# Toeplitz weight blocks loaded once and copied to the second image's rows on GpSimd

## The reference

```python
qkv = _conv(x, w_qkv)                                        # 768 channels
agg = _conv(_conv(qkv, w_dw, groups=C3), w_pw, groups=3 * DIM)
qkv = jnp.concatenate([qkv, agg], axis=1)
...
vk = jnp.einsum('bhds,bhes->bhde', v, k)
out = jnp.einsum('bhde,bhes->bhds', vk, q)
```

## Time and profile before

| | before |
|---|---|
| median of 3 runs | 2079.17 us (2075.14 to 2084.48) |
| profiled execution | 2083.96 us, span of its instructions 2082.1 us |
| PE busy | 1786.3 us (86%) |
| DVE busy | 1372.3 us (66%) |
| ACT busy | 901.7 us (43%) |
| POOL (GpSimd) busy | 277.0 us (13%) |
| mean granted TensorE clock | 0.945 |
| DMA | 267.17 MB in 199916 packets |

### The profile page before, as it was taken

The page is one execution under the profiler, slowest core; times in us unless marked ns, Lnnn a source line. Parts: engine busy times, 40 slices in busy tenths (PEclk is TensorE's granted clock), DMA queues, the critical chain, the costliest instruction groups (busy, mean ns, idle before and its releaser), DMA issues. The chain is left out here.

```text
span 2082.1 us, 42128 instructions
## 1 busy us (share of the span) xinstructions
PE 1786.3 (86%) x16164; PEld 1195.1 (57%) x16164; DVE 1372.3 (66%) x2786; ACT 901.7 (43%) x2341; POOL 277.0 (13%) x189
## 2 busy tenths in 40 slices
PE   2699999999999999997877888999983499999998
PEld 1355555555555555565555666666661366666666
DVE  4677777666555556442333447777875899999994
ACT  0344454454554544453433445455541144444343
POOL 1000000001111101002111110000001233333331
PEclk9899999999999999998988899999995699999999
DMA  3112222237666667479988986545513001111101
GB/s 100 39 63 78 101 94 78 78 125 185 207 170 199 201 160 215 145 185 218 237 231 219 246 229 166 134 121 149 156 48 128 16 32 63 62 63 63 47 32 47
DMA packets 199916, 267.17 MB, mean 128 GB/s; under 512 B 108516, under 2 KB 159588, under 8 KB 199720
## 3 DMA queue, kind: packets, MB, share of 16 engines
q1 hardware_dynamic: 189320, 225.68, 38.4%
q10 hardware_dynamic: 10240, 38.54, 6.0%
q0 software_dynamic: 160, 0.26, 0.0%
HBM read 148.84 MB, written 115.61 MB: 127 GB/s over the span
## 5 line engine op out<-in xcount | busy, mean ns | idle before, releaser
L499 DVE TENSOR_TENSOR vk<-p_vk,mask_vo 128x512 f32<-128x512 f32 x256 | 176.4, 689 | 478.3 <-PE p_vk L392 478.3
L426 PE MATMUL p_dw<-tw,q 98*64 98x98 f32 x3072 | 198.3, 266 | 86.8 <-ACT agg_out L694 34.9
L834 POOL COPY q<-qd 98x768 f32<-98x768 f32 x128 | 110.5, 900 | 1085.5 <-DMA qd<-qkv_scratch 787.2
L667 ACT ACTIVATE half_b<-p_qkv 98x384 f32<-98x384 f32 x256 | 134.2, 524 | 244.2 <-PE p_qkv L351 229.6
L426 PEld LDWEIGHTS p_dw<-tw,q 98*64 98x64 f32 x3072 | 148.1, 143 | 151.5 <-issue 67.8
L694 ACT ACTIVATE agg_out<-p_dw 128x294 f32<-128x294 f32 x256 | 106.9, 417 | 258.6 <-PE p_dw L426 246.0
L452 PE MATMUL p_g<-o,w_proj 128*128 128x392 f32 x512 | 207.5, 531 | 3.4 <-DVE var L555 2.8
L351 PE MATMUL p_qkv<-w_qkv,half_a 128*98 128x384 f32 x512 | 193.8, 502 | 6.7 <-DVE half_a L571 6.7
L351 PE MATMUL p_qkv<-w_qkv,z_odd 128*98 128x384 f32 x512 | 190.2, 494 | 1.8 <-DVE z_odd L571 1.8
L404 PE MATMUL p_out<-vk,qr 128*49 128x136 f32 x2048 | 170.5, 287 | 8.5 <-DVE oN L514 5.4
L711 ACT ACTIVATE o<-p_turn 128x196 f32<-128x196 f32 x256 | 85.5, 334 | 167.5 <-PE p_turn L413 166.1
(11 more groups left out here) (192 smaller groups left out, 3202.4 us busy)
## 6 DMA issues: line engine op xcount, KB each, us to landing
qkv_scratch<-half_b SPq DMA_DIRECT2D x32, 1176.0 KB
qd<-qkv_scratch SPq DMA_DIRECT2D x64, 588.0 KB
agg_scratch<-agg_out ACTq DMA_DIRECT2D x128, 294.0 KB, 5.8
tw<-in_w_toep SPq DMA_DIRECT2D x128, 220.5 KB
half_a<-agg_scratch SPq DMA_DIRECT2D x48, 392.0 KB, 6.9
half_b<-agg_scratch SPq DMA_DIRECT2D x48, 392.0 KB, 6.8
half_a<-in_x SPq DMA_DIRECT2D x16, 784.0 KB, 4.9
x_scratch<-xb SPq DMA_DIRECT2D x16, 784.0 KB, 4.8
```

The source lines that it names most:

```text
L426: mm = pe.matmul(p_dw[NP * cp:NP * cp + NP, PR * s:PR * s + PR], q2[:, U % Q2, DB_CH * cp + 3 * (f % DB_FILLS) + s, :, :].rearrange("r w q ...
L499: v.tensor_tensor(dst[:, :, 0:128].rearrange("p k (c n) -> p k c n", c=HC), src[:, :, 0:2 * D].unsqueeze(2).to_broadcast([128, 4, HC, 2 * D]),
L667: a.activation(raw[:, e, g % 4, :, r], p_qkv[r][0:PR, 0:QKV], ACT.Copy).then_inc(raw_ev, 1)
L834: g.tensor_copy(q2[:, U % Q2, DB_CH * cp:DB_CH * cp + DB_CH, :, :].rearrange("r n w q -> r w n q"), qd[:, :, at:at + DB_CH, :]).then_inc(q ...
```

## The change

The second image's rows move from partitions 49 to 97 to partitions 64 to 112 (P2 = 113), in qd, q2 and tw. The rows 49 to 63 between them are zeroed once in tw and in qd, and the gathers copy the zeros of qd along. tw is loaded for the first image only, by two DMAs instead of four; GpSimd copies it to rows 64 to 112 (`pool_second`) and PE waits for that copy. Each of the four parts of qd is loaded by two DMAs of 49 rows, since its rows are no longer contiguous. GpSimd's order becomes: gather U+2, then the copy for U; at the start of each half three gathers stand ahead of the first copy.

```diff
+P2 = 64 + S
...
-        qd = sb("qd", [PR, NP // 2, QB_CH, 2])
-        q2 = sb("q2", [PR, Q2, 2 * DB_CH, NP // 2, 2])
-        tw = sb("tw", [PR, 2, 2, SB_CH, S])
+        qd = sb("qd", [P2, NP // 2, QB_CH, 2])
+        q2 = sb("q2", [P2, Q2, 2 * DB_CH, NP // 2, 2])
+        tw = sb("tw", [P2, 2, 2, SB_CH, S])
...
-                pe.wait_ge(tw_in[SB % 2], 64 * (SB // 2 + 1))
+                pe.wait_ge(tw_ok, SB + 1)
...
-            sp.dma_start(qd[:, w0:w1, :, :], qt[h][:, w0:w1, QB_CH * qb:QB_CH * qb + QB_CH, :]).then_inc(qd_in, 16)
+            for i in range(2):
+                sp.dma_start(qd[64 * i:64 * i + S, w0:w1, :, :],
+                             qt[h][S * i:S * i + S, w0:w1, QB_CH * qb:QB_CH * qb + QB_CH, :]).then_inc(qd_in, 16)
...
-                g.wait_ge(qd_in, 16 * QD_PARTS * (U // per + 1))
+                g.wait_ge(qd_in, 32 * QD_PARTS * (U // per + 1))
...
-            for i in range(2):
-                for p0, p1 in ((0, S - 1), (S - 1, S)):
-                    sp.dma_start(tw[S * i + p0:S * i + p1, SB % 2, i, :, :],
-                                 ins["w_toep"][p0:p1, SB_CH * sb_:SB_CH * sb_ + SB_CH, :]).then_inc(tw_in[SB % 2], 16)
+            for p0, p1 in ((0, S - 1), (S - 1, S)):
+                sp.dma_start(tw[p0:p1, SB % 2, 0, :, :],
+                             ins["w_toep"][p0:p1, SB_CH * sb_:SB_CH * sb_ + SB_CH, :]).then_inc(tw_in[SB % 2], 16)
+
+        def pool_second(g, SB):
+
+            g.wait_ge(tw_in[SB % 2], 32 * (SB // 2 + 1))
+            wait(g, q2_ok, 2 * min(SB + 3, FILLS // DB_FILLS * (SB // (FILLS // DB_FILLS) + 1)))
+            g.tensor_copy(tw[64:P2, SB % 2, 1, :, :], tw[0:S, SB % 2, 0, :, :]).then_inc(tw_ok, 1)
+            g.wait_ge(tw_ok, SB + 1)
...
-            sp.wait_ge(blank_ok, 1)
+            sp.wait_ge(blank_ok, 2)
...
             g.memset(tw[:, :, :, :, :], 0.0).then_inc(blank_ok, 1)
-            for U in range(2 * FILLS // DB_FILLS):
-                pool_gather(g, U)
+            g.memset(qd[:, :, :, :], 0.0).then_inc(blank_ok, 1)
+            g.wait_ge(blank_ok, 2)
+            per = FILLS // DB_FILLS
+            for U in range(2 * per):
+                if U % per == 0:
+                    pool_gather(g, U)
+                    pool_gather(g, U + 1)
+                if U % per + 2 < per:
+                    pool_gather(g, U + 2)
+                pool_second(g, U)
```

More of the change, by code:

```diff
@@ L262, in layer_one_phase @@
         qd_in, q2_ok = sem("qd_in"), sem("q2_ok")
-        tw_in = [sem("tw_in0"), sem("tw_in1")]
+        tw_in, tw_ok = [sem("tw_in0"), sem("tw_in1")], sem("tw_ok")
         agg_st = [sem("agg_st0"), sem("agg_st1")]
```

## The result

The changed kernel takes 2172.34 us (median of four runs, 2166.09 to 2173.32) against 2080.28 us for the kernel before (2075.14 to 2084.48): a ratio of 1.0455, 95% interval 1.0426 to 1.0484. Slower, as forecast, by 92 us where 142.5 were worked out; the time lies in the stated range of 2125 to 2310 us. The profiled execution spans 2170.9 us against 2082.1, 88.8 us more, and that difference is what the following lines account for.

The account below looks back on a forecast made before the run. PE bounds the first half; in the second, a chain of qd load and the Toeplitz load queued behind it stops PE. Terms 7 + 36 + 14.5 + 71 + 14 = 142.5 us slower gave 2222 us, range 2125 to 2310.

Parts of the forecast that it names:

- Part 3: qd loads: 49-row DMAs use the same seven engines each time, where 98 rows use 14; DMA share about half of 0.97.
- The price of the halving: Each qd load: transfer time doubles at half the engines, +9.9 us, bounds 8.7 and 16.9.
- Second half: Fills 128 to 255: seven chains of qd load, Toeplitz load and copy, 10.2 us longer each, 71 us (54 to 120).
- First half: Fills 0 to 127: longer chains less the distances before, 36 us (20 to 85), plus 14 us for new stalls.
- The clock term: PE in the first half: six new stalls of 3.9 us or more cost 14 us (0 to 20).
- The starts: First products of the halves wait for longer qd load, three gathers and a copy: 7 us and 14.5 us.
- Part 2: GpSimd's copies to the second image's rows: 1.3 us each, bounds 1.0 and 2.4, counting only on the chain.
- part 1: Toeplitz load halved, 220.5 KB less for each of 64 blocks: -1.0 us in each chain, bounds -2.0 and 0.
- The signs: Gather 4Q 25 to 32 us behind first qd issue; second-half PE waits at fill 16Q-8 15 to 20 us.
- (a): qd loads spread evenly or halves on different engines, load as fast as before: +7, 2086 us, no change; chance 0.10.
- (b): As (a), and lighter Toeplitz traffic removes PE's waits in the second half: -30, 2049 us; chance 0.04.
- (c): Seven engines, but the slower qd load mostly hidden, a third of 142.5 us stays: +48, 2127 us; chance 0.06.

Follow-up runs that it names:

- e1: Kernel before, with only each 98-row qd load cut into two of 49 rows, no copy: 2179.02 us, 1.0502.
- e2: Kernel before, with QD_PARTS 8 instead of 4, so as many qd loads as the changed kernel but of 98 rows: 2073.87 us, 0.9986.
- e9: Kernel before, with each qd load cut into 77 and 21 rows: 2114.54 us, 1.0152.
- e6: Kernel before, with each qd load cut into 96 and 2 rows: 2083.56 us, 1.0029.
- e3: Changed kernel, with qd loads cut into 48 + 48 + 2 rows, copy on GpSimd kept: 2094.38 us, 1.0093.
- e5: Changed kernel with 48 + 48 + 2 row qd loads, no copy, both Toeplitz blocks loaded by DMA, GpSimd's order as before: 2090.40 us, 1.0085.
- e4: Changed kernel without the copy: both Toeplitz blocks loaded by DMA, GpSimd's order as before, 49-row qd loads kept: 2173.96 us, 1.0470.

## Why the prediction was right, and where its sizes were off

**Part 3, seven engines: right.** The forecast share of "about half of 0.97" came as 0.49, and e1, e2 and e9 show that neither the count of DMAs nor the copy does it. The trace also counts the engines: the semaphore that qd's loads raise has 960 updates by DMA for the 64 loads before, 15 each, and 1024 for the 128 loads of the changed kernel, 8 each; e9 has 20 for each pair of 77 and 21 rows, e6 19 for 96 and 2, e3 35 for 48, 48 and 2. In the first load before, one update of each DMA comes 0.1 to 0.2 us behind its issue and ahead of its data. Read as that one for a DMA on fewer than 16 engines, and one more for each engine, these counts are 14, 7, 11 + 7, 16 + 2 and 16 + 16 + 2 engines. That both halves use the same seven follows from the rate: 145 GB/s is half of 278. The shares agree with the counts, at 0.07 for each engine: 0.97 for 14 (98 rows), 0.76 for 11 (77 + 21 rows) and 0.49 for 7. When the forecast was made, the trace had only the 0.97 beside 1.07 and 1.14; that 98 rows go to 14 engines and 49 to 7, in equal shares, was my estimate from it, and the counts bear out the numbers of engines. The shares over 1 are overlap in the records, as said there: up to 24 packets run at one time in the stretches of qd alone of e5 and e6, on 16 engines.

**The price of the halving: too high.** The term was +9.9 us a load. Alone it was +8.4 (21.1 against 12.7), below even my lower bound of 8.7; inside the second half, where I had put the upper end at 16.9, it was +7.0 (mean 25.6 against 18.6 of the seven). The term that was mis-sized is the part that doesn't double, put at 2.8 us from a load of 1 KB. By the updates of qd's semaphore the first and the fourth DMA before had landed at 458.58 and 465.00 us, 2.14 us apart for each; four such are 8.6 us of the 12.7, so 4.1 don't double. Doubling 8.6 gives the +8.4 (e1, with nothing but the cut, had +9.5). Inside the second half e1 and e4, which still load both images' blocks, have +8.3 and +8.4 in the mean; the changed kernel's +7.0 is 1.4 less, which fits its lighter Toeplitz traffic but isn't isolated by a run. The upper end of the sum, 17.2 us a chain, was added up from 16.9 and the middle values of the other two parts; by their own bounds it is 19.3, and nothing measured comes near it.

**Second half: 43.5 us for 71.** A group takes 47.4 us instead of 40.3 (fills 144 to 240: 1026.5 to 1310.9 now, 985.5 to 1227.5 before), +7.1 for each of six chains. The seventh, the first in time (fills 128 to 144), grows by 1.1 us only, since the gathers done ahead of the first product let the next qd load be issued 1.7 us behind it instead of 4.8, and its Toeplitz trail is 3.0 us for 4.4. The other terms cancelled as in the sum: the Toeplitz trail behind qd is no longer 1.1 to 5.9 us but 3.0 in five of seven groups, which is the gather and the copy (1.62 and 1.16 us), and 3.6 and 3.7 in the other two (1196.59 to 1200.23 above), where tw landed a little later. The order of GpSimd that I costed at nothing does set this trail, but its mean of 3.2 is that of before.

**First half: 21.6 us for 36 + 14.** The new waits add up to 20.3 us in seven groups (0.0, 7.8, 0.0, 3.4, 7.0, 1.8, 0.3), since the loads grew by 4.8 us in the mean and not by 9.9. The group with the least distance before, 3.3 us, waits 7.0 us, and that with 12.7 us not at all, as the slack says; the second, with 8.4 us, waits most, since its load grew by 10.0 us (16.2 to 26.2). The clock term of 14 us was too high, and no run shows it: the earlier trace rows has one stretch of 7 us at 0.66 behind one stall of 10.0 us, and nothing there or in a run gives what a stall of 3.9 us costs. The runs showed in its place a clock of 0.95 for 0.97 and 6.5 us more of busy PE; the granted clock reads 0.5 for 43.9 us of these products where it read 0.5 for 23.9 before. The same products, fills 0 to 124, before and after:

```profile
473.80:885.40 411.60, 388.33 (x3664) 240.42 (x3658) 231.50 (x500) 203.22 (x481) 50.80 (x56) 0.97 0.65 184
479.90:913.10 433.20, 394.83 (x3658) 244.85 (x3658) 237.12 (x497) 202.68 (x478) 87.22 (x89) 0.95 0.52 158
```

PE is busy 6.5 us longer for the same work at 0.95 for 0.97, and idle 15.1 us longer; the idle time grows by less than the 20.3 us of the new waits, since other short waits shrink. So the chains cost about 15 us for 36 and the slower PE 6.5 for 14. Two of the seven waits were 3.9 us or longer where I had counted six.

**The starts: right.** First product at 479.88 (forecast 481.2), +6.1 for 7; second half +12.2 for 14.5. With the load at 8.4 in place of 9.9 both come out within a microsecond. What the prediction left out is that the first group gives back the order's share of it (e4).

**Part 2, the copy: right.** 1.16 us each, all 64 between 1.162 and 1.296, for 1.3 forecast. e4 shows that it, its order and the lighter traffic of part 1 cancel to within what can be measured. The memset of qd took 5.28 us (5.2 forecast) and cost nothing.

**The signs.** In the second half gather 4Q comes 23.5 to 27.3 us behind the first issue (25 to 32 forecast) and the waits at fill 16Q-8 are 8.2 to 17.5 us (15 to 20 forecast); both are shorter as the load's growth is. No wait of PE for raw stores or agg loads appears among the waits of 470 to 1350 us, as put at nothing.

**Rivals.** (a) and (b) fall with the share of 0.49. (c), a third of the delay, 2127 us, missed by about as much on the other side as the forecast: 62% of the sum was measured.

## What to carry to other kernels

When a buffer is moved so that one wide load becomes several, count the rows of each and what they share evenly among the DMA engines before counting bytes: 49 + 49 rows cost 5.0% here, 48 + 48 + 2 rows under 1%. The bytes that the change saved were worth nothing measurable (e4, which still moves them, has 1.0470, the changed kernel 1.0455). Ask also what is queued behind a load, on the DMA queue and on the engine that waits for it in its own order: here the same 49-row loads cost 5.0% with the Toeplitz loads behind them and 1.7% with those on ACT's queue.

## What the runs showed of the hardware that I had not expected

More engines weren't faster here. Alone on the queues, packets mostly of 768 bytes moved at 145 GB/s with 49-row loads (share 0.49), 278 with 98 rows (0.97), but only 158 to 173 with 48 + 48 + 2 rows (1.13) and 218 with 96 + 2 rows (1.12), where the updates of qd's semaphore count 16 engines; a different row distance in DRAM changed little (180 and 265). Neither the range of rows written nor the row distance explains it, and the cause is open. It mattered less in the loaded stretch: the lone first load took 20.3 us in e3 and 17.9 in e5 (12.7 before), yet the loads in the second half took 18.5 and 19.8 (18.6 before).
